# Closing steps of a fused deformable and grouped bottleneck kernel: part of the residual sums goes from TensorE to VectorE, and a grouped 1x1 convolution and the output ReLUs change places

## What is computed

```python
# layer 0
out    = relu(bn1(conv1x1(x, w1)))              # 1024 -> 256
offset = conv3x3(out, w_off) + b_off            # 256 -> 18
out    = relu(bn2(deform_conv3x3(out, offset, w2)))   # 4 bilinear corners x 9 taps, 256 -> 256
x      = relu(bn3(conv1x1(out, w3)) + x)        # 256 -> 1024
# layer 1, 4 groups, 0/1 mask on 8x8 cells
out = relu(gconv1x1(x * m1, w1)) * m2           # 1024 -> 256
out = relu(gconv3x3(out, w2)) * m2
x   = relu(gconv1x1(out, w3) + x)               # 256 -> 1024, the residual sum of this case
```

## Time and profile before

| | |
|---|---|
| median of 3 runs | 2850.86 us |
| profiled execution | 2852.32 us, its span 2850.5 us, so 1.8 us lie around the span |
| mean granted TensorE clock | 0.993 |
| busy | TensorE 2755.5 us (97%), VectorE 2283.7 us (80%), ScalarE 1225.1 us, GpSimd 1305.0 us |
| identity products L575 | 160 records, first at 2247.4, last at 2845.2 us |
| one closing step with B | 72.85 us, from one `gconv3(0)` (2319.67) to the next (2392.52) |

### The profile page before, as it was taken

How to read it: one execution, slowest core, us unless ns; L and a number is a source line. 1 busy time by engine, 2 the same in 40 slices (tenths; PEclk the granted TensorE clock), 3 DMA queues, 4 the chain that set the end, 5 groups by cost and what they waited for, 6 DMA issues and landing times.

```text
span 2850.5 us, 39431 instructions
## 1 busy us (share of the span) xinstructions
PE 2755.5 (97%) x12960; PEld 1522.4 (53%) x12960; DVE 2283.7 (80%) x5216; ACT 1225.1 (43%) x2466; POOL 1305.0 (46%) x1159
## 2 busy tenths in 40 slices
PE   7978999999999999999999999999999999999998
PEld 3435555555555555555555555555555555555552
DVE  2137888888888888888888888888888888888871
ACT  1114444444444444444444444444444444444442
POOL 2036545444444444444544444454444565555530
PEclk9989999999999999999999999999999999999999
DMA  7779989898888898888989888898988888898861
GB/s 271 222 258 331 323 302 327 322 329 308 311 297 323 326 329 316 315 306 301 325 322 335 310 315 296 313 324 324 332 307 299 295 318 317 316 320 318 316 233 76
DMA packets 263114, 864.37 MB, mean 303 GB/s; under 512 B 31746, under 2 KB 72834, under 8 KB 254336
## 3 DMA queue, kind: packets, MB, share of 16 engines
q0 software_dynamic: 165888, 604.05, 59.8%
q1 hardware_dynamic: 78592, 190.68, 18.9%
q10 hardware_dynamic: 18432, 67.12, 6.0%
HBM read 747.72 MB, written 114.02 MB: 302 GB/s over the span
## 4 chain that ended last, share of the span: by engine, by line
PE 92%; DVE 3%; issue 1%; DMA 1%; POOL 1%; ACT 1%; SPq 0%; DVEq 0%; POOLq 0%; ACTq 0%
PE psR L520 15%; PE psA L409 14%; PE psD L500 9%; PE psV L481 9%; PE psR L552 9%; PE psD L501 9%; PE psD L502 9%; PE psR L569 5%; PE psR L533 4%; PE psA L448 3%; PE psR L575 3%; DVE val L938 1%; DVE y L921 1%; PE psD L448 1%; PE psA L428 1%
## 5 line engine op out<-in xcount | busy, mean ns | idle before, releaser
L374 POOL DMA_INDIRECT corners<-corner_tables,samples_in x1152 | 1290.1, 1120 | 1445.3 <-DVE val L938 993.0
L938 DVE SCALAR_TENSOR_TENSOR val<-corners,samples_in,val 128x256 f32<-128x256 f32 x3456 | 1418.4, 481 | 32.5 <-ACT val L688 30.2
L702 ACT ACTIVATE valT_hi<-psV 128x512 fp32r<-128x512 f32 x576 | 311.5, 593 | 915.5 <-PE psD L502 697.2
L948 DVE TENSOR_TENSOR valT_lo<-psV,valT_hi 128x512 fp32r<-128x512 f32 x576 | 370.9, 686 | 237.2 <-ACT valT_hi L702 221.9
L688 ACT ACTIVATE val<-corners,samples_in 128x256 f32<-128x256 f32 x1152 | 490.4, 503 | 35.6 <-DMA corners<-corner_tables,samples_in 31.5
L500 PE MATMUL psD<-valT_hi,w_hi 128*128 128x512 f32 x1152 | 484.2, 420 | 0.4 <-DVE valT_lo L948 0.4
L520 PE MATMUL psR<-deformed,w_sb 128*128 128x512 f32 x1024 | 463.3, 595 | 2.4 <-ACT y L730 1.9
L501 PE MATMUL psD<-valT_hi,w_lo 128*128 128x512 f32 x1152 | 456.4, 396 | 0.0
L502 PE MATMUL psD<-valT_lo,w_hi 128*128 128x512 f32 x1152 | 455.3, 395 | 0.0
L409 PE MATMUL psA<-x_sb,w_sb 128*128 128x512 f32 x768 | 357.6, 605 | 7.5 <-DMA x_sb<-in_x 7.5
L481 PEld LDWEIGHTS psV<-const_sb,val 128*128 128x128 f32 x2304 | 260.9, 142 | 189.5 <-issue 110.3
(11 more groups left out here) (72 smaller groups left out, 1452.1 us busy)
## 6 DMA issues: line engine op xcount, KB each, us to landing
y<-in_x SPq DMA_DIRECT2D x128, 512.0 KB
out<-y ACTq DMA_DIRECT2D x128, 512.0 KB
x_sb<-in_x SPq DMA_DIRECT2D x48, 1024.0 KB
corner_tables<-x_sb SPq DMA_DIRECT2D x128, 256.0 KB
corners<-corner_tables,samples_in POOLq DMA_INDIRECT x1152
y<-in_x SPq DMA_DIRECT2D x8, 2048.0 KB, 11.4
corner_tables<-corners SPq DMA_DIRECT2D x8, 1139.0 KB, 9.0
samples_dram<-samples SPq DMA_DIRECT2D x32, 90.0 KB
```

What stands on the lines that cost most here:

```text
L374: nc.gpsimd.indirect_dma_start(corners[:, slot, :], None, table, bass.IndirectOffsetOnAxis(ap=index[:, TAPS * t + k:TAPS * t + k + 1], axi ...
L702: nc.scalar.activation(valT_hi[:, m, :], psV[m][:], ACT.Copy).then_inc(valT_ready, 1)
L938: nc.vector.scalar_tensor_tensor(acc, corners[:, n % GS, corner * CMID:(corner + 1) * CMID], samples_in[:, bpar, w:w + 1], acc, ALU.mult, ...
L948: nc.vector.tensor_tensor(valT_lo[:, m, :], psV[m][:], valT_hi[:, m, :].bitcast(F32), ALU.subtract).then_inc(valT_rest, 1)
```

## The change

In the closing steps only: chunks 0, 2 and 4 (the list `ADDED`) get no identity product; VectorE's `out_add` adds the residual, counted by a new semaphore `closing_sum`, and `out_relu` reads `y` for them. TensorE issues `gconv1` behind `turn_val(4)` instead of ahead of `offconv(0)` and `turn_val(4)`. On ScalarE the first two pairs of `out_relu` go from ahead of `valT_copy(7)` and `valT_copy(8)` to behind them, and the third from behind `valT_copy(8)` to the head of `last`, behind `corner0(10)`. On VectorE the first corner of round 4 goes ahead of `ga_mask`; `out_add(0)` stands behind the first corner of round 7, `out_add(2)` behind that of round 8, `out_add(4)` behind `valT_low(8)`.

```diff
+ADDED = [0, 2, 4]
@@ TensorE, gconv3(i) @@
+                    identity = [half for half in range(2) if "A" not in on and 2 * i + half not in ADDED]
                     for half in range(2):
                         rows = slice(64 * half, 64 * half + 64)
                         mm = pe.matmul(psR[half][:], gw3_sb[rows, bank, chunk], gb[rows, bank, :],
-                                       start=True, stop="A" in on)
-                        if "A" in on:
+                                       start=True, stop=half not in identity)
+                        if half not in identity:
                             mm.then_inc(g3_done, 1)
                     if "A" not in on:
-                        for half in range(2):
+                        for half in identity:
                             pe.matmul(psR[half][:], ident, y[:, par, 2 * i + half, :], start=False, stop=True
                                       ).then_inc(g3_done, 1)
...
-                    4: each(gconv1, 0, 1) + each(offconv, 0),
+                    4: each(offconv, 0),
...
                     turn_val(k)
+                    if k == 4 and "A" not in on:
+                        gconv1(0)
+                        gconv1(1)
                     tap(k - 1)
@@ ScalarE, out_relu(m) @@
-                    act.wait_ge(out_sum if "A" in on else g3_done, KC * e + m + 1)
-                    total = y[:, par, m, :] if "A" in on else psR[m % 2][:]
+                    if "A" not in on and m in ADDED:
+                        act.wait_ge(closing_sum, len(ADDED) * (e + LAG_E - NB) + ADDED.index(m) + 1)
+                    else:
+                        act.wait_ge(out_sum if "A" in on else g3_done, KC * e + m + 1)
+                    total = y[:, par, m, :] if "A" in on or m in ADDED else psR[m % 2][:]
...
-                    before = {7: each(out_relu, 0, 1), 8: each(out_relu, 2, 3)}
+                    before = {}
                     after = {
...
-                        8: each(out_relu, 4, 5),
+                        7: each(out_relu, 0, 1),
+                        8: each(out_relu, 2, 3),
                     }
-                    last = each(deformed_relu, 0, 1) + each(out_relu, 6, 7)
+                    last = each(out_relu, 4, 5) + each(deformed_relu, 0, 1) + each(out_relu, 6, 7)
@@ VectorE, out_add(m) and the rounds of a closing step @@
-                    if "E" not in on or "A" not in on:
+                    if "E" not in on:
                         return
                     dve.wait_ge(g3_done, KC * e + m + 1)
                     nc.vector.tensor_tensor(y[:, par, m, :], psR[m % 2][:], y[:, par, m, :], ALU.add
-                                            ).then_inc(out_sum, 1)
+                                            ).then_inc(out_sum if "A" in on else closing_sum, 1)
...
-                    beside[4] += each(ga_mask, 0, 1) + [halo_ga] + c1[4] + c2[4] + c3[4]
+                    beside[4] += c1[4] + each(ga_mask, 0, 1) + [halo_ga] + c2[4] + c3[4]
...
-                    beside[7] += c1[7] + c2[7] + c3[7] + [positions]
-                    beside[8] += c1[8] + c2[8] + each(valT_low, 8) + c3[8] + [coordinates]
+                    beside[7] += c1[7] + each(out_add, 0) + c2[7] + c3[7] + [positions]
+                    beside[8] += c1[8] + each(out_add, 2) + c2[8] + each(valT_low, 8) + each(out_add, 4) + c3[8] + [
+                        coordinates]
```

More of the change, by code:

```diff
@@ L203, in build_program @@
         out_sum = sem("out_sum")
+        closing_sum = sem("closing_sum")
         out_ready = sem("out_ready")
```

## The result

The changed kernel takes 2896.86 us (median of 4 runs, 2894.03 to 2898.73) against 2850.84 before (4 runs): ratio 1.0163, 95% interval 1.0150 to 1.0176. That is 46 us slower; the forecast was 36.5 slower, with a range of 2862 to 2903. The profiled execution takes 2894.03, its span 2892.2.

The account below looks back on a forecast made before the run. TensorE, busy 97% of the span, was taken to bound the kernel. Engine time of +16.1 us and 12 clock falls of +20.4 made +36.5, so 2887.4 us against the median of the runs; range 2862 to 2903.

Parts of the forecast that it names:

- Identity products: TensorE, closing steps: three products of 0.91 us removed per step, saving 2.73 us (bounds 2.7 to 3.0).
- The two waits: TensorE at gconv3(1) and gconv3(2): each waits 2.23 us for output ReLUs behind ScalarE's copy, +4.46 us per step.
- gconv1: TensorE, steps 33 to 39: turn_val(4), now ahead of it, waits for valT_low(3); +1.0 us per step, not -1.78.
- Step 32: The offset convolution ahead of turn_val(4) fills the gap there: -0.9 us; the whole step +0.8 us.
- Steps 40 and 41: Without taps, the four gconv3 follow every 3.1 us in place of 3.73: -3.8 us in all.
- The engine sum: Closing steps by engine time: +19.1 us for steps 33 to 39, +0.8 for step 32, -3.8 at the end: +16.1.
- The clock: TensorE behind 23 new gaps: half taken, 12 falls to 1.2 GHz at 1.70 us each, +20.4 us.
- the clock holds: Rival: no fall of TensorE's clock behind the new gaps, only +16.1 us, 2867 us; chance 0.25.
- The gaps are covered: Rival: ReLUs are done when TensorE reaches gconv3(1) and gconv3(2); the change gains 19.5 us, 2831; chance 0.05.
- Late y: Rival: slower store and load make y_add late, +16 us: 2883 without clock falls, 2903 with them; chance 0.08.

Follow-up runs that it names:

- ScalarE's order alone: The kernel before with only ScalarE's new order of the output ReLUs, all eight identity products kept: 2900.93 us, ratio 1.0175.
- the ReLUs ahead again: The changed kernel with the output ReLUs back ahead of valT_copy(7) and valT_copy(8): 2846.62 us, ratio 0.9995.
- filled run: The changed kernel with two products that nobody reads put into each of three gaps of steps 33 to 39: 2871.10 us, ratio 1.0073.
- sums only: The changed kernel with ReLUs and gconv1 where they were, three VectorE sums still replacing three identity products: 2833.22 us, ratio 0.9942.
- `gconv1` back: The changed kernel with gconv1 ahead of offconv(0) and turn_val(4) again, and ga_mask ahead of the corner: 2880.67 us, ratio 1.0113.
- the move alone: The kernel before with only gconv1 and the first corner of round 4 moved as in the change: 2866.62 us, ratio 1.0057.

## Why the prediction was right, and where it was short

From the first `gconv3` of step 32 to the end the profiled executions take 604.1 (2246.4 to 2850.5) and 650.4 (2241.8 to 2892.2): +46.3. The opening, whose code is the same, came out 3.8 shorter in the second (`conv3(6)` of step 32 at 2206.30 and not 2210.12); from there to the first `gconv3` step 32 is 0.8 shorter by the change. So the change's own cost is +45.5, where the sum said 36.5.

- *Identity products.* From 2401.58 to 2402.54 one now fills 0.96, where two filled 1.82: 0.86 saved each, 0.91 forecast.
- *The two waits.* From the first `gconv3` to the second it is 8.05 where the clock holds, and would be 5.79 without the wait (6.65 before, less 0.86): 2.26, against 2.23. The chain is the one that the prediction wrote down. The run with ScalarE's order alone and the one with the ReLUs ahead again show it from both sides.
- *gconv1.* The mechanism held: `turn_val(4)` is released by `valT_low(3)`, 2.68 after the tap. The filled run gives its size without the clock: 3.08 a step is two waits of 2.25, less 2.58, and 1.16, against 1.0. A step of the run with the ReLUs ahead in which the clock held says the same, 1.17 over the 71.00 of the sums only:

```profile
2460.64:2532.81 72.17, 69.13 (x328) 39.67 (x327) 65.89 (x147) 34.75 (x72) 40.27 (x36) 1.00 0.89 325
```

- *Step 32.* `offconv(0)` fills the gap; 0.75 us of waiting remain ahead of `turn_val(4)`. Saved 0.8, forecast 0.9 (the rows are TensorE's):

```profile
2213.51 1.91 PE L452 MATMUL psA<-mid,woff_sb 128*32 128x512 f32 x16
2216.17 1.16 PE L485 MATMUL psV<-const_sb,val 128*128 128x128 f32 x8 [0.75 <-DVE valT_lo L960]
```

- *Steps 40 and 41.* The four `gconv3` follow each other every 3.05 and not 3.73, forecast 3.1:

```profile
2853.38 1.13 PE L574 MATMUL psR<-gb,gw_sb 64*128 64x512 f32 x4 [1.37 <-DVE gb L925]
2854.44 1.12 PE L580 MATMUL psR<-y,const_sb 128*128 128x512 f32 x2
2856.43 1.13 PE L574 MATMUL psR<-gb,gw_sb 64*128 64x512 f32 x4 [0.87 <-ACT y L741]
```

- *The engine sum.* In the filled run the stretch from the first `gconv3` is 625.2, with one fall left, in step 32. Less 1.7 for that fall this is +19.4 over before; less the 0.8 of step 32 it is 18.6, forecast 16.1. The longer wait at `turn_val(4)` (7 x 0.16) and the product that saves less (24 x 0.05) make most of the 2.5.
- *The clock.* This term was sized too small: 12 falls were forecast, 16 came, 9 behind the sixteen gaps of 2.2 and 7 behind the seven of 2.6 to 2.7, one of them twice as long. The price was right: 9.71 against 8.05 from one `gconv3` to the next where the clock falls between them, 1.66 (1.70 forecast, from eight records, which are four products and not eight). 46.3 less 19.4 leaves 27 for the clock, 1.7 a fall, or 1.6 with the long one counted twice. Half for every gap was the wrong split, as the longer gaps nearly always bring a fall. That the count came within four is in part luck: half was a choice between none and all, and in the other runs the same two kinds of gap brought 9 to 12 falls in 16 and 4 to 7 in 7. "TensorE: Matmul & The Clock Gate" of the Trainium skill, section "A second HAM failure mode: psum-queue depth-cycling", tells of another kernel whose short idle times between groups of products made the clock swing; the trace agrees for 16 of 23 gaps, and not for the rest.

Of the rivals, *the clock holds* (2867) is about what the filled run shows, 2871. Its evidence was weaker than it looked: the gap of 1.94 in step 40 held in the kernel before, and did not in the run with the sums only. *The gaps are covered* is what the run with both orders undone makes of it; the change itself kept them open. *Late y* did not come: `y_add(0)` waits for `conv3`, 3.28 us, and never for a transfer.

## What to carry to other kernels

Work taken from the busiest engine is worth its slot only if what releases that engine next is not made later by the edit: here ReLUs moved behind a copy that waits for the tap, and transposes moved ahead of what had covered their wait, turned a gain of 18 us into a loss of 46. Look up on the other queue, by name, what stands between the end of the preceding work and the releaser. And cost a gap on TensorE twice, once for its length and once for the clock behind it; where a gap can't be closed, work that nobody needs can be cheaper than idling, as the filled run is by 26 us.

## What was not expected of the hardware

How often the clock falls behind a gap turns sharply within one microsecond. Counted by the granted clock in steps 32 to 39 of these profiles: behind gaps of 1.8 (before, `gconv1` back, sums only, ScalarE's order alone) 0 of 32; behind those of 2.1 to 2.2 (changed, `gconv1` back, ScalarE's order alone) 30 of 48; behind those of 2.6 to 2.7 (changed, ReLUs ahead, the move alone) 18 of 21. Behind the gap of 1.9 ahead of `gconv2` in step 40 it fell in 3 of all 12 profiles. Like gaps of one run differ, and the same gap in other runs. That the length alone decides isn't shown: each length has its own place in the step, with other work around it. Two products that nobody reads, 1.88 us by their timeline in each gap, took 26 us off the kernel.
